# A two-layer graph and expert kernel: the rows of an expert tile are turned by VectorE in 32 by 32 blocks

## The reference, cut to what matters

```python
logits = xt @ Wr + br                      # 8 experts, the top 2 of a node are used
xn = layernorm(xt)
xe = xn * ln_g[e] + ln_b[e]                # layer 1 only: each expert has a scale and shift of its own
h  = gelu(xe @ W1[e] + b1[e])              # 256 -> 1024   (layer 0: 256 -> 512)
y  = h @ W2[e] + b2[e]                     # back to 256
out = sum over the 2 chosen experts of weight * y
```

## Time and profile before

| | us |
|---|---|
| time before, median of 3 runs | 1894.77 (1891.58 to 1897.01) |
| time of the profiled execution | 1897.33 |
| its span, first to last instruction | 1895.6 |
| PE busy | 1667.7 (88%) |
| ACT busy | 999.7 (53%) |
| DVE busy | 966.4 (51%) |
| POOL busy | 327.4 (17%) |
| expert stage of layer 0 | about 507 to 752 |
| expert stage of layer 1 | about 1449 to 1892 |

### The profile page before, as it was taken

The page is one execution under the profiler, slowest core; times in us unless marked ns, Lnnn a source line. Parts: engine busy times, 40 slices in busy tenths (PEclk is TensorE's granted clock), DMA queues, the critical chain, the costliest instruction groups (busy, mean ns, idle before and its releaser), DMA issues. The chain is left out here.

```text
span 1895.6 us, 41585 instructions
## 1 busy us (share of the span) xinstructions
PE 1667.7 (88%) x13046; PEld 1523.3 (80%) x13073; DVE 966.4 (51%) x2257; ACT 999.7 (53%) x2110; POOL 327.4 (17%) x282
## 2 busy tenths in 40 slices
PE   4799999997599998385998989989875999999998
PEld 3588787785489997364998989989855999999997
DVE  4678777884511221577887868866765101011111
ACT  1233443545055554016989979889741445545453
POOL 2100000000156665000000000000001333333332
PEclk9899999998699999698999999999987999999999
DMA  9980000103377876500000000000064666666663
GB/s 158 108 153 9 9 9 17 45 9 123 134 177 200 200 199 156 166 0 20 18 10 16 14 13 18 8 18 17 4 243 184 186 175 185 179 181 184 177 189 95
DMA packets 88054, 189.86 MB, mean 100 GB/s; under 512 B 13193, under 2 KB 62857, under 8 KB 79145
## 3 DMA queue, kind: packets, MB, share of 16 engines
q1 hardware_dynamic: 51785, 138.33, 22.1%
q0 software_dynamic: 30608, 45.56, 15.9%
q10 hardware_dynamic: 5584, 4.99, 0.8%
HBM read 188.98 MB, written 33.11 MB: 117 GB/s over the span
## 5 line engine op out<-in xcount | busy, mean ns | idle before, releaser
L1495 PE MATMUL bank<-arena 128*128 128x195 bf16 x5408 | 473.2, 249 | 42.3 <-DVE arena L1352 42.3
L1495 PEld LDWEIGHTS bank<-arena 128*128 128x128 fp8e4 x5408 | 468.5, 98 | 47.0 <-issue 45.5
L1257 ACT ACTIVATE arena<-arena,m_row 128x512 fp8e5<-128x512 f32 (+1 forms) x672 | 401.5, 678 | 64.6 <-DVE arena L1352 43.8
L2050 DVE TENSOR_TENSOR arena<-bank,X 128x256 f32<-128x256 f32 x118 | 50.1, 425 | 578.4 <-PE bank L1991 578.4
L1953 PEld LDWEIGHTS bank<-X,arena 128*128 128x128 f32 x2832 | 338.7, 194 | 6.0
L1953 PE MATMUL bank<-X,arena 128*128 128x128 f32 x2832 | 339.2, 277 | 0.0
L1991 PE MATMUL bank<-arena,X 128*128 x1416 | 329.2, 383 | 5.5 <-ACT X L2026 2.6
L1126 PE MATMUL bank<-arena 128*128 (+1 forms) x1352 | 313.5, 387 | 17.7 <-DVE arena L1031 15.4
L1126 PEld LDWEIGHTS bank<-arena 128*128 128x128 f32 x1352 | 253.4, 192 | 58.3 <-issue 23.2
L1991 PEld LDWEIGHTS bank<-arena,X 128*128 128x128 f32 x1416 | 260.9, 191 | 43.3 <-issue 12.3
L985 ACT ACTIVATE bank<-arena,s_all 128x384 f32<-128x384 f32 (+1 forms) x234 | 133.7, 573 | 188.9 <-DVE arena L1023 183.9
(11 more groups left out here) (220 smaller groups left out, 1332.4 us busy)
## 6 DMA issues: line engine op xcount, KB each, us to landing
arena<-m1w SPq DMA_DIRECT2D x67, 1024.0 KB, 4.8
arena<-m0w SPq DMA_DIRECT2D x67, 512.0 KB, 4.3
xs<-X SPq DMA_DIRECT2D x4, 1664.0 KB, 6.7
arena<-qd SPq DMA_DIRECT2D x25, 256.0 KB, 3.2
arena<-adjT POOLq DMA_DIRECT2D x13, 448.0 KB, 12.9
arena<-adjT POOLq DMA_DIRECT2D x13, 384.0 KB, 10.8
xe<-zeros POOLq DMA_DIRECT2D x1, 3456.0 KB, 21.6
X<-x_in SPq DMA_DIRECT2D x2, 1664.0 KB, 11.2
```

The source lines that it names most:

```text
L1257: last = a.activation(self.sign[slot].bitcast(F8W)[:, q * W:q * W + nt * P], self.row[r][:, 0:nt * P], ACT.Sigmoid, scale=STEEP, bias=self ...
L1495: last = pe.matmul(bank[rb * NT + n][:, kind * KW:(kind + 1) * KW], self.split[slot][kind].bitcast(F8)[:, q * W + n * P:q * W + (n + 1) * ...
```

## The change

PE no longer turns the rows. DVE does, in a new `turn_x` of sixteen instructions for each tile: each reads 32 partitions of `rx[q]` (one quarter) and, for both halves at once (a 32 x 2 x 32 access), 32 columns, turns the two 32 by 32 squares and writes them to the quarter of the target that the columns belong to. The inner loop steps through the target's quarters, the outer one through the source's. So all of bank 4's turning is gone.

In layer 0 the target is `rxt[s]` itself, and ACT's copy is gone: PE waits for `tx_ready` where it waited for `xgt_ready`, and DVE waits for `h_ready` of tile g before it overwrites `rxt[s]` for tile g+2. In layer 1 the target is a new buffer `turned[s]`, and ACT still applies scale and shift, from SBUF now instead of from PSUM.

DVE's order becomes turn(0), turn(1), and then turn(g+2), tile(g) for each g; its loop body holds four tiles instead of two.

```diff
+                self.turned = ring(2, D) if second_norm else self.rxt
...
             def tiles_tensor(self, pe):
+                kept = self.xgt_ready if self.second_norm else self.tx_ready
...
-                def turn_x(q):
-                    for k in range(KC):
-                        last = pe.transpose(bank[4][:, k * P:(k + 1) * P], self.rx[q][:, k * P:(k + 1) * P],
-                                            ident[:, :])
-                    last.then_inc(self.tx_ready[q % 2], 1)
...
                     if left >= 1:
                         pe.wait_ge(self.w1_loaded[o], 16 * (i + s + 1))
-                        pe.wait_ge(self.xgt_ready[o], i + s + 2)
+                        pe.wait_ge(kept[o], i + s + 2)
                         pe.wait_ge(self.ht_ready[o], i + s + 1)
                         hidden(o)
-                    if left >= 2:
-                        pe.wait_ge(self.rx_loaded[(q + 2) % 4], 16 * (j + 1 + (q >= 2)))
-                        turn_x((q + 2) % 4)
...
                 def keep_x(g, s):
-                    if not self.second_norm:
-                        a.copy(self.rxt[s], bank[4][:, 0:D]).then_inc(self.xgt_ready[s], 1)
-                        return
                     e = a.value_load(expert_of[0:1, at(g, 1)], min_val=0, max_val=E - 1)
                     for k in range(KC):
-                        last = a.activation(self.rxt[s][:, k * P:(k + 1) * P], bank[4][:, k * P:(k + 1) * P],
+                        last = a.activation(self.rxt[s][:, k * P:(k + 1) * P], self.turned[s][:, k * P:(k + 1) * P],
...
-                    if more:
+                    if more and self.second_norm:
                         a.wait_ge(self.tx_ready[s], i + 3)
                         keep_x(2 * i + s + 2, s)
...
             def tiles_vector(self, v):
+                def turn_x(j, q):
+                    i, s = 2 * j + q // 2, q % 2
+                    if not isinstance(j, int) or 4 * j + q >= 2:
+                        if self.second_norm:
+                            v.wait_ge(self.xgt_ready[s], i + 1)
+                        else:
+                            v.wait_ge(self.h_ready[s], i + 1)
+                    v.wait_ge(self.rx_loaded[q], 16 * (j + 1))
+                    to = self.turned[s].rearrange("p (k r) -> p k r", k=KC)
+                    of = self.rx[q].rearrange("p (k d) -> p k d", k=KC)
+                    for rq in range(0, P, 32):
+                        for dq in range(0, P, 32):
+                            last = v.transpose(to[dq:dq + 32, :, rq:rq + 32], of[rq:rq + 32, :, dq:dq + 32])
+                    last.then_inc(self.tx_ready[s], 1)
...
+                def four(j):
+                    for q in range(4):
+                        turn_x(j + q // 2, (q + 2) % 4)
+                        tile(2 * j + q // 2, q % 2)
```

More of the change, by code:

```diff
@@ L1956, in hidden @@
                     last.then_inc(self.h_ready[s], 1)
-                def turn_x(q):
-                    for k in range(KC):
-                        last = pe.transpose(bank[4][:, k * P:(k + 1) * P], self.rx[q][:, k * P:(k + 1) * P],
-                                            ident[:, :])
-                    last.then_inc(self.tx_ready[q % 2], 1)
[L1964 to L1968, removed]
+                pe.wait_ge(kept[0], 2)
                 pe.wait_ge(self.w1_loaded[0], 16)
@@ L2014, in keep_x @@
                     last.then_inc(self.xgt_ready[s], 1)
-                for s in range(2):
-                    a.wait_ge(self.tx_ready[s], 2)
-                    keep_x(s, s)
+                if self.second_norm:
+                    for s in range(2):
+                        a.wait_ge(self.tx_ready[s], 2)
+                        keep_x(s, s)
                 a.wait_ge(self.b_loaded, 32)
@@ L2041, in tiles_vector @@
             def tiles_vector(self, v):
+                def turn_x(j, q):
+                    i, s = 2 * j + q // 2, q % 2
+                    if not isinstance(j, int) or 4 * j + q >= 2:
+                        if self.second_norm:
+                            v.wait_ge(self.xgt_ready[s], i + 1)
[8 more added lines that the diff above has]
+                    last.then_inc(self.tx_ready[s], 1)
+                for q in range(2):
+                    turn_x(0, q)
                 v.wait_ge(self.b_loaded, 32)
@@ L2054, in tile @@
                                     ).then_inc(self.ry_ready[s], 1)
[L2056 to L2061, removed]
+                def four(j):
+                    for q in range(4):
+                        turn_x(j + q // 2, (q + 2) % 4)
+                        tile(2 * j + q // 2, q % 2)
+                assert RUN_TILES % 4 == 3
+                four(0)
+                with v.Fori(1, RUN_TILES // 4) as j:
+                    four(j)
+                j = RUN_TILES // 4
+                turn_x(j, 2)
+                for q in range(3):
+                    tile(2 * j + q // 2, q % 2)
         def layer_norm_stats(v, sems, nth=1, done=False):
```

## The result

The changed kernel takes 1951.1 us (median of 4 runs, 1949.11 to 1953.79) against 1894.55 for the kernel before (4 runs). The ratio is 1.030 with a 95% interval of 1.028 to 1.032: slower by 3%. The forecast was 1963, in a range from 1912 to 2018. The profiled execution has a span of 1950.9 us where that of before had 1895.6, so 55.3 us have to be found.

The account below looks back on a forecast made before the run. PE was taken to set the pace of both layers, with room on DVE. Layer 0 tiles +70, its start +1, layer 1 tiles -6, its start +3 make +68 on 1897.3: 1965, or 1963 for a median, range 1912 to 2018.

Parts of the forecast that it names:

- The cost of a turn: On DVE, each of sixteen turns a tile takes 0.25 us from start to start, 4.0 us together.
- its two reasons: Why DVE's turns wouldn't overlap: each must read all 32 columns before writing a first one, and each writes another quarter.
- The first two rivals: DVE's turns overlap (under 0.14 to 0.15 each, 1863, chance 0.13) or half overlap (up to 0.20, 1885 to 1925, chance 0.08).
- DVE as the bound of layer 0: In layer 0 DVE needs 5.2 us a tile against PE's 3.50, costing 1.28 for each of about 55 tiles: +70 us.
- the value load: In layer 0's tile on DVE, a value load between operations, partly beside the last turns, adds 0.25 us (0 to 0.5).
- The hand-over: In layer 0's tile on DVE, a hand-over adds 0.05 us to the sum of 5.2.
- The ends of layer 0: At layer 0's start the first turn takes 4.0 us, but the bias load holds ACT there anyway: +1 us.
- Layer 1: DVE isn't the bound; late y in one tile of two leaves 0.10 of 0.22 us gained a tile: -6, start +3.
- The sum: Whole kernel, against the profiled execution's 1897.3: +70 + 1 - 6 + 3 = +68 us, so 1965, or 1963 for a median.
- The ends of the range: Whole kernel: 1918 with 0.22 a turn and no value-load gap; 2025 with 0.28 and a gap of 0.5.
- The clock rival: In layer 0, PE's gaps drop the granted clock to 1.2 GHz: +60 us on top, about 2025; chance 0.07.
- Rival 1: DVE's turns overlap, a layer 0 tile takes 3.5 us and layer 1 gains all 0.22: -34 us, 1863; chance 0.13.

Follow-up runs that it names:

- eight: The changed kernel with every second square left out, so eight turns a tile instead of sixteen (rows not the reference's): 1875.13 us, one run.
- eight_half_load: Against eight, each layer 0 load of W1 after the first two and before the last brings half its columns (stale weights): 1861.14 us, one run.

## Why the prediction was right, step by step

**The cost of a turn was right, for one of its two reasons.** The forecast took 0.25 us from start to start. Measured: 3.98 us for sixteen, 0.249 each. The reason that held is the change of quarter. The other one, that a turn must read all 32 columns before it writes and so can't overlap the next, fell: inside a quarter turns overlap too, with starts 0.13 apart where copies have 0.10. Some of the precision is luck: the line through the earlier trace rows gives 0.26 at 64 elements, and those rows have a semaphore between them, which the turns don't. The first two rivals, turns that overlap or half overlap, fell; the first one's price of 0.14 was close to what turns without a change of quarter do (0.13).

**DVE as the bound of layer 0 was right; the tile was 0.3 too long.** Predicted 5.2, measured 4.92 in the mean: 4.82 in three tiles of four and 5.20 in the fourth. The term of the sum that was mis-sized is the value load, put at 0.25 with 0 and 0.5 as ends. It costs 0.03: the last turn ends at 644.30 and the next operation starts at 644.33, so the load runs beside the turns. The hand-over, put at 0.05 after the end of the multiplication, is negative: the first turn starts 0.27 after the start of that operation (644.88 to 645.15), which lasts 0.35. A term was missing: the end of DVE's loop body, 0.38 once in four tiles, 0.1 for a tile. So layer 0's tiles cost 55 us and not 70. In the kernel with turns inside quarters the value load does show, with 0.34 of idle time in front of the addition:

```profile
607.96 0.42 DVE L2057 TENSOR_TENSOR arena<-bank,X 128x256 f32<-128x256 f32 x1 [0.34 <-issue]
```

There turns follow each other too fast to cover it.

**The ends of layer 0.** Put at +1 us in all; measured -2.0 at the start and +0.5 at the end. The first turns do take 4.0 us each, but the clock was already high at the first y, which the forecast didn't consider.

**Layer 1: right in mechanism, short in size.** The account foresaw keep_x ending 6.77 after the end of y(g-1), and it ends 1663.30 - 1656.52 = 6.78 after it. Its terms were off by 0.1 or so and cancel: DVE starts 0.26 and not 0.16 after y, the turn 0.82 and not 0.95 after that, and keep_x takes 0.88 and not 0.81, since each of its two activations lasts 486 ns from SBUF and 454 did from PSUM. It foresaw y(g+1) 0.24 late in each pair; that is 0.19. What it didn't have is the 0.25 by which a y that had to wait is longer. Together 0.44 are lost in each pair, all of the gain, where 0.24 had left 0.10 for each tile. So the -6 became -0.5. The start was put at +3 and cost 3.1.

**The sum.** Forecast for the profiled execution +70 + 1 - 6 + 3 = +68; measured +55.3 - 1.5 - 0.5 + 3.1, less 1.1 elsewhere, = +55.3. The two errors of size, 15 too much in the tiles of layer 0 and 5.5 too little in those of layer 1, have opposite signs, so the total is nearer than its largest term. The ends of the range, 1918 and 2025, were added to the profiled execution's time and not to the median, which makes them 2.5 us too high.

**The clock rival fell.** PE is busy for 77% of layer 0 and waits 1.1 us for each tile, and its clock stays at 1.00.

**What the forecast had wrong without being asked.** Rival 1 priced layer 0 at 3.50 us a tile once the turns are cheap. The runs eight and eight_half_load show that the loads of W1 stop it at about 3.75, so 1863 could not have been reached by cheaper turns alone. The forecast had set these loads aside, which is right at 4.9 us a tile, but the rival spoke of 3.5.

## What to carry to other kernels

Moving work to an engine that is idle for 80% pays only if its operations are long: 0.22 us of PE became sixteen operations with 0.25 us each. On DVE, operations that hop between partition quarters don't overlap. No order of the sixteen avoids that in a whole turn: each joins another pair of source and target quarter, so every step changes at least one of the two. What helps is to make them deeper (128 elements cost 0.315 instead of 0.249). Before counting a gain on the bounding engine, look at who is next: here first ACT's hand-over, cured by turning one tile earlier, and then the weight loads. And once an engine is the bound, count what its own loop costs at its end; while it waited for others, that was hidden.

## What the runs showed of the hardware

Not expected: a change of quarter on the source side alone or the target side alone costs the same, and a plain copy is held by it like a turn. A held operation starts 0.01 us after the end of the one before, for turns of 64 elements (0.236 and 0.249) and of 128 (0.303 and 0.316). A value load of 0.3 us on DVE's queue is free behind sixteen operations that each wait for the last, and costs 0.34 behind sixteen that overlap. The end of a loop body on DVE costs 0.38 us where DVE is the bound. And a pause on PE costs more than its own length: y loses the 0.16 us by which it overlaps hidden and lasts 3.71 us instead of 3.62, at the same granted clock.
